# The end of a batch-norm attention stage: where the denominators' transforms stand on TensorE, and unused full-height transposes between them

## The reference, cut to what matters

```python
q, k, v = x @ Wq + bq, x @ Wk + bk, x @ Wv + bv
score = softmax(einsum('bnd,bmd->bnm', q, k) / 64, axis=2)
h = einsum('bnm,bmd->bnd', score, v) @ Wl + bl
mean = jnp.mean(h, axis=(0, 1))
var = jnp.mean((h - mean) ** 2, axis=(0, 1))
y = jax.nn.relu((h - mean) * jax.lax.rsqrt(var + 1e-5) * gamma + beta)
return y + x
```

## Time and profile before

| | |
|---|---|
| median of 3 runs | 698.66 us (698.52 to 698.70) |
| the profiled execution | 692.95 us, with a span of 691.0 us from its first to its last instruction |
| mean granted clock | 0.925 |
| PE busy | 585.3 us, 85% of the span |
| DVE, ACT, POOL busy | 486.1, 310.5, 252.3 us |

### The profile page before, as it was taken

How to read it: one execution, slowest core, us unless ns; L and a number is a source line. 1 busy time by engine, 2 the same in 40 slices (tenths; PEclk the granted TensorE clock), 3 DMA queues, 4 the chain that set the end, 5 groups by cost and what they waited for, 6 DMA issues and landing times. The chain is left out here.

```text
span 691.0 us, 13147 instructions
## 1 busy us (share of the span) xinstructions
PE 585.3 (85%) x4778; PEld 385.8 (56%) x4778; DVE 486.1 (70%) x1352; ACT 310.5 (45%) x659; POOL 252.3 (37%) x220
## 2 busy tenths in 40 slices
PE   6995777978876979899899999998697979988886
PEld 5774666756643523222587877887132233987453
DVE  0455667867466796888647888587757898954695
ACT  1431433745556534355234655323232438943174
POOL 6756971131002210110175686553301138800150
PEclk9998898999985599999999999999897999999998
DMA  6877622020000200000100000004000010000002
GB/s 187 237 249 200 186 67 81 3 66 0 1 1 0 83 0 1 0 1 0 42 8 8 15 9 8 15 1 135 17 1 0 1 42 1 2 3 2 0 1 62
DMA packets 18944, 30.06 MB, mean 44 GB/s; under 512 B 6466, under 2 KB 15810, under 8 KB 18242
## 3 DMA queue, kind: packets, MB, share of 16 engines
q1 hardware_dynamic: 16322, 19.81, 10.1%
q0 software_dynamic: 2560, 9.44, 4.7%
HBM read 27.26 MB, written 1.05 MB: 41 GB/s over the span
## 5 line engine op out<-in xcount | busy, mean ns | idle before, releaser
L177 POOL TENSOR_TENSOR norm_rstd<-norm_var,minus_half 128x16 f32<-128x16 f32 x16 | 47.1, 2943 | 174.5 <-DVE norm_var L171 174.5
L1413 ACT ACTIVATE m_g<-PS,w_slot 128x512 f32<-128x512 f32 x96 | 60.8, 685 | 85.2 <-PE PS L1464 85.2
L1358 DVE TENSOR_TENSOR m_gw<-m_g,PS 128x512 f32<-128x512 f32 x96 | 60.9, 675 | 16.7 <-PE PS L1472 7.9
L1464 PE MATMUL PS<-m_xT,w_slot 64*128 64x512 f32 x192 | 61.9, 653 | 0.7 <-ACT m_g L1413 0.5
L1488 PE MATMUL PS<-m_gw,w_slot 128*64 128x512 f32 x192 | 56.1, 654 | 1.2 <-DVE m_gw L1358 1.2
L106 PE MATMUL PS<-w_base 128*128 128x128 f32 x350 | 51.5, 296 | 5.6 <-DMA w_base<-in_w_base 4.2
L106 PEld LDWEIGHTS PS<-w_base 128*128 128x128 f32 x350 | 43.0, 152 | 12.6 <-issue 5.7
L1472 PE MATMUL PS<-m_gT,m_sel 48*128 48x512 bf16 x96 | 24.8, 409 | 18.6 <-DVE m_gw L1358 15.0
L147 DVE BATCH_NORM_STATS2 norm_halves<-H 128x6 f32<-128x64 f32 x256 | 34.6, 211 | 3.4 <-PEq L2906 3.1
L1472 PEld LDWEIGHTS PS<-m_gT,m_sel 48*128 48x128 bf16 x96 | 5.9, 93 | 53.1 <-DVE m_gw L1358 41.3
L262 POOL DMA_INDIRECT tok_windows<-in_emb,tok_ids x32 | 30.5, 953 | 11.2 <-issue 9.4
(11 more groups left out here) (341 smaller groups left out, 1489.8 us busy)
## 6 DMA issues: line engine op xcount, KB each, us to landing
rff_routed<-in_routed SPq DMA_DIRECT2D x64, 129.0 KB, 2.5
w_slot<-in_w_rat SPq DMA_DIRECT2D x1, 1525.0 KB, 10.9
w_slot<-in_w_win SPq DMA_DIRECT2D x1, 1378.5 KB, 6.0
w_slot<-in_w_m SPq DMA_DIRECT2D x1, 1329.0 KB, 5.7
w_slot<-in_w_early SPq DMA_DIRECT2D x1, 1100.0 KB, 5.0
rat_inv<-in_rat_taps SPq DMA_DIRECT2D x1, 1024.0 KB, 7.6
rat_hf<-in_rat_taps SPq DMA_DIRECT2D x1, 1024.0 KB, 8.0
out<-H SPq DMA_DIRECT2D x8, 128.0 KB, 2.2
```

The lines of the kernel that those rows point to most:

```text
L177: nc.gpsimd.tensor_tensor(N.rstd[:], N.var[:], C.minus_half[:], ALU.pow).then_inc(S["norm_rstd"], 1)
L1358: nc.vector.tensor_tensor(gw[:, i % 2, half, :], g[:, i % 2, half, :], gate_bank[half], ALU.mult)\
L1413: nc.scalar.activation(g[:, i % 2, half, :], hid_bank[(n - 1) % 3], ACT.Gelu, bias=b1[:, s:s + 1])\
L1464: nc.tensor.matmul(hid_bank[n % 3], w1[lane(half), s, :], pair_of(xT, pair)[lane(half)], start=True, stop=True).then_inc(S["hid_ps"], 1)
```

## The change

D2 moves from between sum1 and sum2 to behind the spread, and D3 from ahead of the last turning to behind D2. Then PE waits for the mean and issues eight unused transposes into a free part of the bank with the sums, ahead of the first turning. After each of the turnings 1 to 6 it issues one more. After D4 and again after D5 it issues eight; the four after D5 are gone. ACT, DVE, POOL and SP issue what they issued, in the same order.

```diff
@@ -1091,7 +1091,6 @@
             nc.tensor.matmul(PS[0][:, 0, 0:1], halves[lower, 0, :], running[:, CHUNKS:], start=True, stop=True)\
                 .then_inc(S["sum1_ps"], 1)
             denominators(1)
-            denominators(2)
             pe.wait_ge(S["sum2"], 1)
@@ -1099,9 +1098,12 @@
             nc.tensor.matmul(PS[0][:, 0, 4:5], halves[:, 2, :], both[:, 0:1], start=True, stop=True)\
                 .then_inc(S["spread_ps"], 1)
+            spare = PS[0][:, 0, P:]
+            denominators(2)
+            denominators(SQUARED_FIRST)
+            pe.wait_ge(S["bn_mean"], 1)
+            rouse(nc, C, spare, 8)
             for c in range(CHUNKS):
-                if c == CHUNKS - 1:
-                    denominators(SQUARED_FIRST)
                 pe.wait_ge(S["y"], c + 1)
@@ -1109,9 +1111,11 @@
                 ins.then_inc(S["y_ps"], 1)
+                if 1 <= c < CHUNKS - 1:
+                    rouse(nc, C, spare, 1)
             for s in range(4, SQUARED_TAIL):
                 denominators(s)
-            rouse(nc, C, PS[0][:, 0, :], 4)
+                rouse(nc, C, spare, 8)
```

## The result

The changed kernel takes 699.7 us (median of 20 executions, 697.3 to 704.2), the kernel before 698.11 us next to it (20 executions, 693.3 to 701.2). The ratio is 1.0038 with a 95% interval of 1.0020 to 1.0056, that is +2.65 us (1.4 to 3.9). A repeat with 12 executions gave 1.0033 (1.0007 to 1.0058), or +2.3 us. So it is slower, by two thirds of the 3.97 us that were forecast (by the medians, two fifths).

The account below looks back on a forecast made before the run. Bound: first add, statistics, last turning, D4, D5, move of D5, at clock 0.50. Of +3.97 us, 1.89 come from ahead of the last turning, the rest from transposes between D4 and D5: 702.6 us, own range 701.3 to 703.9, wide 699.0 to 704.0.

Parts of the forecast that it names:

- the rival with the clock up from D4 on: Stage's end and next opening: clock stays up through D4 and D5, -0.2 to +2.0 us, 698.4 to 700.7; chance 0.20.
- D2 away from sum2, a gain that is lost again: Sums: sum2 starts 1.0 us earlier, but ACT moves D2 ahead of its first ReLU, which starts near 210.8, not 209.93.
- D3 and eight transposes ahead of the first turning, 1.8: PE ahead of the first turning: D3 and eight transposes make that turning start 1.8 us later.
- One transpose after each of the turnings, 0.1: Turnings 1 to 6: turning plus transpose takes 0.70 us against DVE's 0.60 per chunk; a loss of 0.1 us.
- D3 gone from the last turning, nothing: Ahead of the last turning: D3 lay in PE's idle time under DVE's statistics, so its removal changes nothing.
- Eight transposes between D4 and D5, 1.8 to 2.1: Stage's end: ACT waits 2 us for D5 behind the transposes, a loss of 1.8 to 2.1 us.
- I take the clock as it is in the rows, 0.50 from 202 on: Premise of the sum: clock at 0.50 from 202 on, since up to D1 both kernels issue the same.
- the clock up already at D2 and D3: Rival: clock already up while D2 and D3 run; gain of 0.8 us, 2.1 with the opening, 696.5 us; chance 0.10.
- The transposes never raise the clock: Rival: clock stays at 0.50 throughout, the time is that of the sum, 702.6 us; no separate chance given.
- Later stages fall differently: Rival: later stages fall differently against the clock's changes, 1 us either way; chance of worse than 703.9 us 0.09.

Follow-up runs that it names:

- the late move: The kernel before with D2 behind the spread on PE and its move on ACT behind the last ReLU, no new transposes: 695.16 us, ratio 0.9972.
- the order alone: The changed kernel's order of sums, D2, D3 and turnings with none of the added transposes, four at the end as before: 696.6 us, ratio 0.9978.
- the run with a filled pause: The changed kernel with sixteen transposes instead of one behind turning 6, ahead of the last turning: 697.3 us, ratio 0.9984.

## Why the prediction was right in kind and too large

The median of 699.7 us lies inside the wide range, 699.0 to 704.0, but 2.9 us under the 702.6 and under the forecast's own range, which starts at 701.3; by the ratio, with +2.65 us, it is just at that end. As a median it falls where the prediction had put the rival with the clock up from D4 on (698.4 to 700.7), whose mechanism no trace of the changed kernel shows in full. So it is the marks of the stage's end, and not the time, that speak for the prediction. The 5.71 us by which the first profiled execution lay under the median do not come from the stage's end: the second trace of the kernel before, at 698.28 us, is 5.3 us longer, 1.8 of it ahead of D0 and 3.6 behind the first row of the next stage's gates, with the part between them 0.1 shorter.

*D2 away from sum2, a gain that is lost again*: right. Sum2 starts when DVE's total is there, 0.5 to 1.2 us earlier than before. The first ReLU stands behind D2's move all the same, 0.6 to 1.3 late. The run with the late move has the gain without the loss.

*D3 and eight transposes ahead of the first turning, 1.8*: right in kind, between +2.1 (first trace) and +1.5 (the two others), since the clock fell inside D0 in the first trace (D0 took 1.58 us, not 1.13) and behind it in the others.

*One transpose after each of the turnings, 0.1*: nothing in any of the three. The statistics are 2.1, 1.4 and 1.4 late, as much as the first turning.

*D3 gone from the last turning, nothing*: right by itself, since that turning still waits for DVE. The prediction also expected the clock to fall in the gap that D3 had filled, and the runs bear that out: with D3 or sixteen transposes in the pause the clock stayed up through D5.

*Eight transposes between D4 and D5, 1.8 to 2.1*: this and the one for the first turning are the terms that were mis-sized. From D4's start to D5's it is 3.9, 3.5 and 3.2 us in the three traces, against nearly 1.9 before, so a loss of 2.0, 1.7 and 1.4. D4 runs partly at 1.00 in two of them, which I had allowed for in the forecast's own range and not in its sum.

The weak step is the sentence "I take the clock as it is in the rows, 0.50 from 202 on". With it I took one trace's clock as the kernel's. The clock's rise and fall do not lie at a fixed place of the stage: in three traces of one kernel the stretch at 1.00 lies 14.2 to 17.6, 11.7 to 18.5 and 11.9 to 18.8 us behind D0. The first trace agrees with my marks within 0.5 us and has the next stage's load at +4.1; the other two at +2.9 and +2.6. That the first one came so close is thus in part luck. The mean of the three loads, 26.9 against 23.7, is +3.2, and the next stage's gates are late by as much (33.6 against 30.4). The whole time has +2.65 (1.4 to 3.9) and +2.3 (0.5 to 4.1). The 0.6 to 0.9 us between them lie inside the intervals. But all the timed runs point the same way: each whole time lies 0.1 to 2.1 us under what the load of its own trace would give, most of all with the order alone (-1.5 us against +0.6). Single traces cannot tell if later stages give this back, since from the first row of the gates to the program's end it is 459.6 and 463.1 us in the two of the kernel before and 460.3 to 464.2 in the three of the changed one. It stays open.

The rivals: *the clock up already at D2 and D3* fell, with 0.50 through both in every trace of the changed kernel. PE was busy 9.47 of 10.10 us there. The Trainium skill's "TensorE: Matmul & The Clock Gate", section "Why this matters for your kernels", would have the clock up in such a stretch; the trace disagrees, as it did in the kernel before. *The transposes never raise the clock* fell too: it rises 10.7 to 14.9 us behind D0 in all nine traces with added transposes, and in the four without (the kernel before twice, the order alone, the late move) it is 0.50 until 38.6 us or later. The Trainium skill's section "Part 4: PE-mode transpose" on the same page, by which transposes do not count as PE being busy for the clock, is not borne out by these runs with f32. *The clock stays up through D4 and D5* did not come true here, but the run with a filled pause shows that its mechanism exists, and D4 ran partly at 1.00 in two traces. *Later stages fall differently* can't be told from the spread of single executions.

## What to carry to other kernels

Put filler work where its engine waits anyway. Here eight transposes cost nothing ahead of a turning that waited for ACT, and 0.7 us or nearly their whole length where the path ran through them. And look at what follows the filler: the same 30 transposes stood in a slower kernel where a pause behind them let the clock fall again, and in one that was not slower where real work filled that pause. Moving a step on one engine moves its consumer's place on another, so look at what stands behind that consumer in its own order. And where the clock changes inside the stage, take the sum at both levels from more than one trace, because one execution shows one placing only.

## What the hardware showed that I had not expected

One kernel's executions differ by several us without any change: the kernel before lay between 690 and 703 us over all sets, with D0 at 201.04 in one trace and 202.85 in another. The granted clock changes at other places of the stage each time (for the changed kernel, the rise 11.7, 11.9 or 14.2 us behind D0), and the length of rows changes with it, D4 between 1.40 and 2.08 us. What makes the place differ was not tried.
